# First weight block loaded in two transfers, and one zero multiplication fewer ahead of it, in a two-layer LoRA residual kernel

## The chip, the cores and the metric

The kernel runs on one core of one Trainium2 chip. The metric is device time in microseconds (us) of one execution; lower is better. A core has TensorE (matrix multiplications; weight loads are listed apart, as PEld), VectorE (DVE), ScalarE (ACT), GpSimd (POOL) and SyncE (SP), whose queue issues most of the transfers here.

## What is computed

Two linear layers follow each other, each with a residual and a low-rank correction that is chosen per batch entry by an index (8 batch entries, 256 tokens, width 1024, float32):

```python
base = einsum('bti,oi->bto', x, W0) + b0
x    = x + base + 2 * einsum('btr,bro->bto', einsum('bti,bir->btr', x, A0[idx0]), B0[idx0])
base = einsum('bsd,od->bso', x, W1) + b1
x    = x + base + einsum('bsr,bor->bso', einsum('bsd,brd->bsr', x, A1[idx1]), B1[idx1])
```

## The kernel before, in words

The kernel first multiplies the two weights with each other, (1 + W0) times (1 + W1) in effect, and then applies the product to the tokens of each of the 8 batch entries. Both large products are cut into quadrants of 512 x 512 and combined by sums and differences of quadrants, so that seven quadrant products do instead of eight. The quadrants of the first weight are called u11, u12, u21, u22, those of the second v11 to v22; us3, vt3 and the like are their sums and differences. Every operand is held as a high part (rounded to the format that TensorE multiplies, written by ScalarE as a CAST, "hi") and a low part (the remainder, written by VectorE as a subtraction, "lo"), and a product takes three passes: high x high (line 1127), high x low (line 1131) and low x high (line 1132).

Quadrants u11 and v11 come first, in four blocks k = 0 to 3 of 128 rows x 512 columns (256 KB). The SP queue issues, one after the other, v11 block 0 (line 327), u11 block 0 (line 328), blocks 1 to 3 of both (line 331), then u12, v21 in two halves, u21, v22, v12, u22 (lines 336 and 339). In each block of u11 and v11 the unit matrix has to be added to the 128 x 128 piece on the diagonal. For block 0 this is spread out by hand:

- VectorE (lines 701 to 713) adds the unit matrix to the first 128 columns of v11 and then of u11, once into the high operand (line 707) and once into the raw block (line 708). Then it makes the low parts of v11 and u11, one instruction of 512 columns each (line 712).
- ScalarE (lines 463 to 467) rounds the other 384 columns of v11, then those of u11, into the high operands.
- TensorE (lines 1165 to 1170) fills the time until the data are there with multiplications of zeros: 4 of 128 columns (line 1167), then WARM = 6 of 512 columns (line 1170). Its first real multiplication (row group m = 0, line 1127) waits for the third of the four diagonal additions, m = 1 to 3 wait for ScalarE's part of u11, and the eight low passes of block 0 (lines 1131, 1132) wait for both low parts.

Blocks 1 to 3 go through lines 699 (diagonal), 472 (high) and 718 (low). VectorE's program is one strict list. After the low parts of u12 and of half of v21 it waits for the transfer of u21 (line 941) and makes us3 = u21 - u11 (line 731, combine). Then follow, among others, the low part of the rest of v21, the diagonal of v22, the low part of an adapter factor (line 736, which waits for ScalarE's line 484), vt3, and all low parts up to that of v22 (line 728). TensorE waits for the low part of v22 after it has turned a block by four transposes (line 1153), at the third quadrant product (line 1229). Semaphore counts are kept in `hi` and `lo`, per place; `filled(q, n)` gives the count at which n parts of q are there, from the table PARTS.

Of the kernel before, what the change touches and what calls it, by code (L numbers as in the profile page):

```python
# [8 lines left out]
ALU = mybir.AluOpType  # L9

P = 128
HALF = 512
WARM = 6
WARM_SHORT = 4
DMA = 16

KH = 4
# [10 lines left out]
SLOT = {"u11": 0, "v11": 1, "u12": 2, "v21": 3, "us3": 4, "vt3": 5, "us4": 0, "v22": 2, "us2": 4, "vt2": 0,  # L28
        "us1": 1, "u22": 3, "vt1": 5, "vt4": 2, "d11": 0, "t3": 4, "t2": 5, "d21": 1, "t1": 3, "t4": 2, "d22": 6}


REST = ("12", "21", "22")
PARTS = {"u11": KH, "v11": KH, "u12": 2, "v21": 2, "d21": KH, "d22": KH}


A11, A21, A12, A22, S1, S2, S3, S4 = range(8)
# [3 lines left out]

def lora_pair(nc, xT, U11, V11, W0, W1T, A0, B0T, A1T, B1, b0, b1, idx0, idx1, out):
    B, _, _, QW = xT.shape

    TILES = 4
# [19 lines left out]
    with ExitStack() as ctx:  # L64
# [3 lines left out]
        def sem(name):  # L68
            return ctx.enter_context(nc.semaphore(name))
# [66 lines left out]
        def raw(name):  # L136
            at = UNIT[name]
            return raw_a[:, at, :] if at < 4 else raw_b[:, at - 4, :]

        def raw_k(name, k, n=1):  # L140
            return raw(name)[:, k * HALF:(k + n) * HALF]

        def op(name, part):
            return ops[:, SLOT[name], part, :]

        def op_k(name, part, k, n=1):
            return op(name, part)[:, k * HALF:(k + n) * HALF]
# [48 lines left out]

        warm_set = sem("warm_set")
        landed = {q: sem(f"landed_{q}") for q in ("u12", "u21", "u22", "v12", "v22")}
        v21_landed = [sem(f"landed_v21_{n}") for n in range(KH // GROUP)]
        first_landed = {q: [sem(f"landed_{q}_{g}") for g in range(KH)] for q in ("u11", "v11")}  # L200
        lora_landed = sem("lora_landed")
# [18 lines left out]
        diag_added = sem("diag_added")  # L220
# [4 lines left out]
        hi = [sem(f"hi_of_place{s}") for s in range(7)]  # L225
        lo = [sem(f"lo_of_place{s}") for s in range(7)]
# [57 lines left out]
        def filled(q, n):  # L284

            ahead = list(SLOT)[:list(SLOT).index(q)]
            return n + sum(PARTS.get(p, 1) for p in ahead if SLOT[p] == SLOT[q])

# [4 lines left out]
        def _(sp):  # L293
# [30 lines left out]
                             ).then_inc(stored[name], DMA)  # L324


            sp.dma_start(raw_k("v11", 0), V11[0, :, :]).then_inc(first_landed["v11"][0], DMA)
            sp.dma_start(raw_k("u11", 0), U11[0, :, :]).then_inc(first_landed["u11"][0], DMA)
            for k in range(1, KH):
                for q, src in (("u11", U11), ("v11", V11)):  # L330
                    sp.dma_start(raw_k(q, k), src[k, :, :]).then_inc(first_landed[q][k], DMA)
# [130 lines left out]
        def _(act):  # L462
            def first_block():

                for q in ("v11", "u11"):
                    act.wait_ge(first_landed[q][0], DMA)
                    nc.scalar.copy(op_k(q, 0, 0)[:, P:HALF], raw_k(q, 0)[:, P:HALF]).then_inc(hi[SLOT[q]], 1)

            def high_first(k):
                for n, q in enumerate(("u11", "v11")):  # L470
# [78 lines left out]
            act.dma_start(idx[0:1, B:2 * B], idx1).then_inc(idx_landed, DMA)  # L549
            act.dma_start(idx[0:1, 0:B], idx0).then_inc(idx_landed, DMA)  # L550
            first_block()
            for k in range(1, KH):
                high_first(k)
# [132 lines left out]
        def _(dve):  # L686
# [14 lines left out]
            def first_block():  # L701

                dve.wait_ge(ident_made, 2)
                for q in ("v11", "u11"):
                    dve.wait_ge(first_landed[q][0], DMA)
                    block = raw_k(q, 0)[:, 0:P]
                    nc.vector.tensor_tensor(op_k(q, 0, 0)[:, 0:P], block, ident[:, :], ALU.add).then_inc(diag_added, 1)  # L707
                    nc.vector.tensor_tensor(block, block, ident[:, :], ALU.add).then_inc(diag_added, 1)
                for n, q in enumerate(("v11", "u11")):
                    dve.wait_ge(diag_added, 2 * n + 2)  # L710
                    dve.wait_ge(hi[SLOT[q]], 1)
                    nc.vector.tensor_tensor(op_k(q, 1, 0), raw_k(q, 0), op_k(q, 0, 0), ALU.subtract
                                            ).then_inc(lo[SLOT[q]], 1)

            def low_first(k):
                for q in ("u11", "v11"):
                    dve.wait_ge(hi[SLOT[q]], filled(q, k + 1))
                    nc.vector.tensor_tensor(op_k(q, 1, k), raw_k(q, k), op_k(q, 0, k), ALU.subtract
                                            ).then_inc(lo[SLOT[q]], 1)

# [9 lines left out]
            def combine(q, left, right, how):  # L730
                nc.vector.tensor_tensor(raw(q), raw(left), raw(right), how).then_inc(summed[q], 1)  # L731
# [200 lines left out]
            nc.vector.memset(bias_sum, 0.0).then_inc(zeroed, 1)  # L932
            nc.vector.memset(t_cols[:, :], 0.0).then_inc(zeroed, 1)
            first_block()
            for k in range(1, KH):
                diagonal(k)
                low_first(k)
# [1 line left out]
            low_half("u12", 2)  # L939
            low_half("v21", 0)  # L940
            dve.wait_ge(landed["u21"], DMA)
            dve.wait_ge(lo[SLOT["u11"]], filled("u11", KH))
            combine("us3", "u21", "u11", ALU.subtract)
            low_half("v21", 2)
            add_diagonal("v22", diag_v22)
# [173 lines left out]
        def _(pe):  # L1119
# [6 lines left out]
            def high_pass(u, v, bank, m, k, on_top=False):  # L1126
                return mm(bank[:, :], left(u, 0, k, m), op_k(v, 0, k), start=(k == 0 and not on_top), stop=False,  # L1127
                          skip_group_check=on_top)

            def low_passes(u, v, bank, m, k, on_top=False):  # L1130
                mm(bank[:, :], left(u, 0, k, m), op_k(v, 1, k), start=False, stop=False, skip_group_check=on_top)  # L1131
                return mm(bank[:, :], left(u, 1, k, m), op_k(v, 0, k), start=False, stop=(k == KH - 1),  # L1132
                          skip_group_check=on_top)
# [34 lines left out]
            pe.wait_ge(warm_set, 2)  # L1168
            for _ in range(WARM):
                mm(banks[7][:, :], c_rows[:, 0:P], c_rows[:, 0:HALF], start=True, stop=True)  # L1170


            for k in range(KH):
                if k == 0:

                    pe.wait_ge(diag_added, 3)
                else:
                    pe.wait_ge(hi[SLOT["u11"]], filled("u11", k + 1))
                pe.wait_ge(hi[SLOT["v11"]], filled("v11", k + 1))
                if k < KH - 1:  # L1180
                    for m in range(KH):
                        if k == 0 and m == 1:
                            pe.wait_ge(hi[SLOT["u11"]], filled("u11", 1))
                        high_pass("u11", "v11", a_banks[m], m, k)
                pe.wait_ge(lo[SLOT["u11"]], filled("u11", k + 1))
                pe.wait_ge(lo[SLOT["v11"]], filled("v11", k + 1))
                for m in range(KH):
                    if k == KH - 1:

                        high_pass("u11", "v11", a_banks[m], m, k)  # L1190
                    last = low_passes("u11", "v11", a_banks[m], m, k)
                    if k == KH - 1:
                        last.then_inc(m_done[1], 1)
# [58 lines left out]
            for h in range(NH):  # L1252
                cols = slice(h * HALF, (h + 1) * HALF)
# [235 lines left out]
```

## Time and profile before

| | |
|---|---|
| median of 3 runs | 282.63 us (282.19 to 282.70) |
| the profiled execution, its own time | 281.97 us |
| its span, first to last instruction | 280.4 us |
| TensorE busy | 276.3 us, 99% of the span |
| VectorE busy | 214.5 us, 77% |
| ScalarE busy | 102.0 us, 36% |
| mean granted TensorE clock | 0.999 |

The page sums up one execution. The busy time of TensorE contains the zero multiplications. Of the 281.97 us, 1.57 lie outside the span. The timeline lists instructions by start and duration; a bracket at the end of a line gives the idle time of that engine just before, and what ended it.

### The profile page before, as it was taken

The numbers are of one execution on the slowest core, as the hardware profiler recorded it, in microseconds if no ns is written. First come the engines' busy times: TensorE is split into PE (matmuls) and PEld (weight loads), VectorE is DVE, ScalarE is ACT, GpSimd is POOL, SyncE is SP. The second block draws the span as 40 slices with busy tenths as digits, with TensorE's granted clock in tenths as the row PEclk, the third lists the DMA queues.
The fourth block names the chain that finished last, engine by engine and source line by source line (L and its number), as shares of the span: only waits on it lengthen the run. The fifth ranks groups of instructions, "written<-read, shape, count | busy, mean of one in ns | idle before, by whom it ended". The sixth has DMA issues, their size and how long they took to land.

```text
span 280.4 us, 3861 instructions
## 1 busy us (share of the span) xinstructions
PE 276.3 (99%) x1321; PEld 225.4 (80%) x1321; DVE 214.5 (77%) x321; ACT 102.0 (36%) x141; POOL 19.2 (7%) x45
## 2 busy tenths in 40 slices
PE   8999999999999999999999999999999999999995
PEld 6888888888888886888877888888877888888885
DVE  5779999999899799798972875875772865875413
ACT  4665465352964665404131223132311223132000
POOL 3333200400000001001000000000000000000000
PEclk9999999999999999999999999999999999999999
DMA  7997100200476200383702703703802302203003
GB/s 245 388 411 287 37 1 2 57 19 0 150 269 247 86 2 19 109 314 126 248 15 84 247 29 121 240 6 124 236 1 86 125 0 112 95 2 132 19 0 150
DMA packets 13112, 33.93 MB, mean 121 GB/s; under 512 B 2165, under 2 KB 2421, under 8 KB 13094
## 3 DMA queue, kind: packets, MB, share of 16 engines
q1 hardware_dynamic: 12066, 31.60, 31.8%
q0 software_dynamic: 1024, 2.10, 2.3%
q8 instruction: 10, 0.16, 0.2%
q14 instruction: 8, 0.07, 0.1%
q10 hardware_dynamic: 4, 0.00, 0.0%
HBM read 22.09 MB, written 11.60 MB: 120 GB/s over the span
## 4 chain that ended last, share of the span: by engine, by line
PE 99%; DVE 0%; issue 0%
PE bank L1291 18%; PE bank L1292 18%; PE bank L1293 18%; PE bank L1127 9%; PE bank L1131 9%; PE bank L1132 9%; PE bank L1323 3%; PE bank L1298 3%; PE bank L1159 1%; PE bank L1161 1%; PE bank L1160 1%; PE bank L1147 1%; PE bank L1146 1%; PE bank L1145 1%; PE bank L1170 1%; PE bank L1238 1%
## 5 line engine op out<-in xcount | busy, mean ns | idle before, releaser
L1291 PE MATMUL bank<-ops,late 128*128 128x512 f32 x192 | 75.1, 391 | 0.0
L1292 PE MATMUL bank<-ops,late 128*128 128x512 f32 x192 | 74.8, 390 | 0.0
L1293 PE MATMUL bank<-ops,late 128*128 128x512 f32 x192 | 74.7, 389 | 0.0
L1131 PE MATMUL bank<-ops 128*128 128x512 f32 x112 | 43.8, 391 | 0.0
L1132 PE MATMUL bank<-ops 128*128 128x512 f32 x112 | 43.6, 390 | 0.0
L1291 PEld LDWEIGHTS bank<-ops,late 128*128 128x128 f32 x192 | 36.1, 188 | 8.7 <-issue 1.2
L1293 PEld LDWEIGHTS bank<-ops,late 128*128 128x128 f32 x192 | 36.0, 188 | 7.6
L1292 PEld LDWEIGHTS bank<-ops,late 128*128 128x128 f32 x192 | 36.1, 188 | 7.4
L1127 PE MATMUL bank<-ops 128*128 128x512 f32 x112 | 40.9, 400 | 0.0
L525 ACT CAST late<-rows 128x512 fp32r<-128x512 f32 x24 | 14.7, 620 | 54.7 <-DVE rows L823 29.5
L1127 PEld LDWEIGHTS bank<-ops 128*128 128x128 f32 x112 | 21.5, 192 | 4.7 <-DVE ops L707 0.3
L1132 PEld LDWEIGHTS bank<-ops 128*128 128x128 f32 x112 | 21.2, 189 | 4.5
L1131 PEld LDWEIGHTS bank<-ops 128*128 128x128 f32 x112 | 21.2, 189 | 4.5
L728 DVE TENSOR_TENSOR ops<-raw_a,ops 128x2048 fp32r<-128x2048 f32 x9 | 20.6, 2284 | 0.0
L802 DVE TENSOR_TENSOR late<-rows,late 128x512 fp32r<-128x512 f32 x24 | 16.5, 690 | 4.9 <-ACT late L525 4.8
L479 ACT CAST ops<-raw_a 128x2048 fp32r<-128x2048 f32 x9 | 17.1, 1911 | 7.4 <-DVE raw_a L731 4.6
L909 DVE TENSOR_TENSOR raw_a<-bank,raw_a 128x512 f32<-128x512 f32 x8 | 5.5, 692 | 17.7 <-PE bank L1298 17.6
L479 ACT CAST ops<-raw_b 128x2048 fp32r<-128x2048 f32 x6 | 11.4, 1915 | 6.3 <-DVE raw_b L731 3.7
L728 DVE TENSOR_TENSOR ops<-raw_b,ops 128x2048 fp32r<-128x2048 f32 x6 | 13.6, 2286 | 0.0
L897 DVE TENSOR_TENSOR raw_a<-bank,raw_a 128x512 f32<-128x512 f32 x8 | 5.5, 690 | 8.4 <-PE bank L1293 8.4
L802 DVE TENSOR_TENSOR late<-raw_a,late 128x512 fp32r<-128x512 f32 x15 | 10.1, 687 | 2.0 <-ACT late L525 1.9
L547 ACT COPY raw_a<-bank 128x512 f32<-128x512 f32 x4 | 2.3, 587 | 24.0 <-PE bank L1298 24.0
(175 smaller groups left out, 397.4 us busy)
## 6 DMA issues: line engine op xcount, KB each, us to landing
out<-raw_a SPq DMA_DIRECT2D x27, 256.0 KB, 2.3
raw_a<-xT SPq DMA_DIRECT2D x10, 512.0 KB, 6.8
a<-rb_rows SPq DMA_DIRECT2D x8, 392.0 KB
x_mid<-xT SPq DMA_DIRECT2D x6, 512.0 KB, 6.3
raw_b<-W SPq DMA_DIRECT2D x2, 1024.0 KB, 16.2
rb_rows<-b_hl SPq DMA_DIRECT2D x3, 512.0 KB
rb_rows<-late SPq DMA_DIRECT2D x3, 512.0 KB
raw_b<-V SPq DMA_DIRECT2D x4, 256.0 KB, 3.7
```

The lines of the kernel that those rows point to most:

```text
L479: nc.scalar.copy(op(q, 0), raw(q)).then_inc(hi[SLOT[q]], 1)
L525: nc.scalar.copy(x_op(j, 0), x_raw(j, b)).then_inc(op_hi[j], 1)
L728: nc.vector.tensor_tensor(op(q, 1), raw(q), op(q, 0), ALU.subtract).then_inc(lo[SLOT[q]], 1)
L802: nc.vector.tensor_tensor(x_op(j, 1), x_raw(j, b), x_op(j, 0), ALU.subtract).then_inc(op_lo[j], 1)
L1127: return mm(bank[:, :], left(u, 0, k, m), op_k(v, 0, k), start=(k == 0 and not on_top), stop=False, skip_group_check=on_top)
L1131: mm(bank[:, :], left(u, 0, k, m), op_k(v, 1, k), start=False, stop=False, skip_group_check=on_top)
L1132: return mm(bank[:, :], left(u, 1, k, m), op_k(v, 0, k), start=False, stop=(k == KH - 1), skip_group_check=on_top)
L1291: mm(bank[:, :], hi, t_op(t, 0, k), start=(start and k == 0), stop=False, skip_group_check=not start)
L1292: mm(bank[:, :], hi, t_op(t, 1, k), start=False, stop=False, skip_group_check=not start)
L1293: last = mm(bank[:, :], lo, t_op(t, 0, k), start=False, stop=(k == KH - 1), skip_group_check=not start)
L1298: return mm(bank[:, :], h_stack[b % 2][0:STACK, q * P:(q + 1) * P], rb[b % 2][:, h * HALF:(h + 1) * HALF], start=False, stop=True, skip_gr ...
L1323: last = mm(bank[j * CT:(j + 1) * CT, 0:T], of_b[:, k, :], xr[at][kh][:, :, tok], start=(k < TILES), stop=(k >= KT - TILES))
```

## The change

The transfer of u11 block 0 becomes two: columns 0 to 127 (64 KB, 512 bytes of each row) by itself, and then columns 128 to 511 (192 KB) with a semaphore of their own. WARM goes from 6 to 5. ScalarE's high part of u11 block 0 becomes two instructions (128 and 256 columns), and so does VectorE's low part (256 and 256 columns). TensorE waits for the first piece before m = 1 and for the second before m = 2. u11 now has five parts instead of four, and the counts that others wait for are raised to match.

```diff
-WARM = 6
+WARM = 5
...
-PARTS = {"u11": KH, "v11": KH, "u12": 2, "v21": 2, "d21": KH, "d22": KH}
+PARTS = {"u11": KH + 1, "v11": KH, "u12": 2, "v21": 2, "d21": KH, "d22": KH}
...
+        u11_rest_landed = sem("u11_rest_landed")
...
             sp.dma_start(raw_k("v11", 0), V11[0, :, :]).then_inc(first_landed["v11"][0], DMA)
-            sp.dma_start(raw_k("u11", 0), U11[0, :, :]).then_inc(first_landed["u11"][0], DMA)
+            for cols, done in ((slice(0, P), first_landed["u11"][0]), (slice(P, HALF), u11_rest_landed)):
+                sp.dma_start(raw_k("u11", 0)[:, cols], U11[0, :, cols]).then_inc(done, DMA)
...
-                for q in ("v11", "u11"):
-                    act.wait_ge(first_landed[q][0], DMA)
-                    nc.scalar.copy(op_k(q, 0, 0)[:, P:HALF], raw_k(q, 0)[:, P:HALF]).then_inc(hi[SLOT[q]], 1)
+                for q, done, cols in (("v11", first_landed["v11"][0], slice(P, HALF)),
+                                      ("u11", u11_rest_landed, slice(P, 2 * P)),
+                                      ("u11", u11_rest_landed, slice(2 * P, HALF))):
+                    act.wait_ge(done, DMA)
+                    nc.scalar.copy(op_k(q, 0, 0)[:, cols], raw_k(q, 0)[:, cols]).then_inc(hi[SLOT[q]], 1)
...
-                for n, q in enumerate(("v11", "u11")):
-                    dve.wait_ge(diag_added, 2 * n + 2)
-                    dve.wait_ge(hi[SLOT[q]], 1)
-                    nc.vector.tensor_tensor(op_k(q, 1, 0), raw_k(q, 0), op_k(q, 0, 0), ALU.subtract
-                                            ).then_inc(lo[SLOT[q]], 1)
+                for q, parts, cols in (("v11", 1, slice(0, HALF)), ("u11", 1, slice(0, 2 * P)),
+                                       ("u11", 2, slice(2 * P, HALF))):
+                    dve.wait_ge(diag_added, 2 if q == "v11" else 4)
+                    dve.wait_ge(hi[SLOT[q]], parts)
+                    nc.vector.tensor_tensor(op_k(q, 1, 0)[:, cols], raw_k(q, 0)[:, cols], op_k(q, 0, 0)[:, cols],
+                                            ALU.subtract).then_inc(lo[SLOT[q]], 1)
...
-                    dve.wait_ge(hi[SLOT[q]], filled(q, k + 1))
+                    dve.wait_ge(hi[SLOT[q]], filled(q, k + 1 + PARTS[q] - KH))
...
-            dve.wait_ge(lo[SLOT["u11"]], filled("u11", KH))
+            dve.wait_ge(lo[SLOT["u11"]], filled("u11", PARTS["u11"]))
...
-                    pe.wait_ge(hi[SLOT["u11"]], filled("u11", k + 1))
+                    pe.wait_ge(hi[SLOT["u11"]], filled("u11", k + 2))
                 pe.wait_ge(hi[SLOT["v11"]], filled("v11", k + 1))
                 if k < KH - 1:
                     for m in range(KH):
-                        if k == 0 and m == 1:
-                            pe.wait_ge(hi[SLOT["u11"]], filled("u11", 1))
+                        if k == 0 and m in (1, 2):
+                            pe.wait_ge(hi[SLOT["u11"]], filled("u11", m))
                         high_pass("u11", "v11", a_banks[m], m, k)
-                pe.wait_ge(lo[SLOT["u11"]], filled("u11", k + 1))
+                pe.wait_ge(lo[SLOT["u11"]], filled("u11", k + 2))
```

## Rows read from the trace of the kernel before

**Rows 1.** The page, part 4: the chain that ended last, by engine.
```profile
PE 99%; DVE 0%; issue 0%
```

**Rows 2.** The waits of TensorE's weight loads, whole span: us in total, times, longest.
```profile
PEld bank L1167 <- DVE c_rows L931: 1.3, 1, 1.3
PEld bank L1291 <- issue: 1.2, 3, 0.4
...
PEld bank L1127 <- DVE ops L707: 0.3, 1, 0.3
```

**Rows 3.** The timeline, first 9 us, TensorE: start, duration, instruction, idle before.
```profile
2.22 2.87 PE L1170 MATMUL bank<-c_rows 128*128 128x512 f32 x6
4.65 1.42 PEld L1127 LDWEIGHTS bank<-ops 128*128 128x128 f32 x4 [0.29 <-DVE ops L707]
4.88 1.91 PE L1127 MATMUL bank<-ops 128*128 128x512 f32 x4
6.59 0.59 PE L1131 MATMUL bank<-ops 128*128 128x512 f32 x1
7.02 0.39 PE L1132 MATMUL bank<-ops 128*128 128x512 f32 x1
7.25 0.39 PE L1131 MATMUL bank<-ops 128*128 128x512 f32 x1
```

**Rows 4.** The timeline, 1 to 7 us: SP, VectorE and ScalarE around block 0.
```profile
1.43 0.42 SPq L328 DMA_DIRECT2D raw_a<-U  x1
3.66 0.51 ACT L467 CAST ops<-raw_b 128x384 fp32r<-128x384 f32 x1 [0.60 <-DMA raw_b<-V]
3.73 0.29 DVE L707 TENSOR_TENSOR ops<-raw_b,ident 128x128 fp32r<-128x128 f32 x1 [1.00 <-DMA raw_b<-V]
3.94 0.28 DVE L708 TENSOR_TENSOR raw_b<-raw_b,ident 128x128 f32<-128x128 f32 x1
4.31 0.29 DVE L707 TENSOR_TENSOR ops<-raw_a,ident 128x128 fp32r<-128x128 f32 x1
...
5.32 0.68 DVE L712 TENSOR_TENSOR ops<-raw_a,ops 128x512 fp32r<-128x512 f32 x1
6.24 0.62 ACT L472 CAST ops<-raw_a 128x512 fp32r<-128x512 f32 x1 [1.42 <-DVE raw_a L699]
```

**Rows 5.** Issue to landing: block 0 of v11 (line 327) and of u11 (line 328).
```profile
DMA to landing us min/median/max: 2.6/2.6/2.6
DMA to landing us min/median/max: 2.9/2.9/2.9
```

**Rows 6.** The page, part 6: a transfer of 64 KB: count, size, us to landing.
```profile
a_raw<-A POOLq DMA_DIRECT2D x8, 64.0 KB, 2.0
```

**Rows 7.** Windows: stretch, length, busy per engine, clock, transfer engines' share, GB/s.
```profile
3.00:4.00 1.00, 1.00 (x3) 0.74 (x3) 0.27 (x2) 0.40 (x2) 0.00 (x0) 1.00 1.03 383
12.00:14.00 2.00, 2.00 (x10) 1.65 (x10) 1.46 (x2) 1.99 (x3) 0.77 (x2) 1.00 1.04 422
```

**Rows 8.** The waits of VectorE, 0 to 60 us: total, times, longest.
```profile
DVE raw_a L731 <- DMA raw_b<-W: 1.5, 1, 1.5
DVE ops L718 <- ACT ops L472: 1.5, 3, 0.5
...
DVE ops L723 <- ACT ops L476: 0.5, 1, 0.5
DVE a L736 <- ACT a L484: 0.3, 1, 0.3
```

**Rows 9.** The timeline: u21's transfer, and VectorE's work from its landing to v22.
```profile
6.20 0.46 SPq L339 DMA_DIRECT2D raw_b<-W  x1
18.09 2.29 DVE L731 TENSOR_TENSOR raw_a<-raw_b,raw_a 128x2048 f32<-128x2048 f32 x1 [1.50 <-DMA raw_b<-W]
42.05 2.28 DVE L728 TENSOR_TENSOR ops<-raw_a,ops 128x2048 fp32r<-128x2048 f32 x1
```

**Rows 10.** The timeline, weight loads: the four transposes and the load behind them, twice.
```profile
43.78 0.58 PEld L1153 LDWEIGHTS bank<-ident,g_all 128*128 128x128 f32 x4
44.40 0.19 PEld L1127 LDWEIGHTS bank<-ops 128*128 128x128 f32 x1
102.26 0.58 PEld L1153 LDWEIGHTS bank<-ident,g_all 128*128 128x128 f32 x4
102.81 0.19 PEld L1127 LDWEIGHTS bank<-ops 128*128 128x128 f32 x1
```

## The prediction

> **What bounds the kernel now.** I read the page's chain first: it is TensorE for 99% of the span [rows 1]. So a change is worth what it does to the moment at which TensorE finishes its list. The waits of the weight loads say where that list is held up: 1.3 us at the very start for the first zeros, 0.3 us ahead of the first real multiplication, and a few pauses with no releaser [rows 2]. Seen this way nothing else holds TensorE, and a zero multiplication taken out in front should come off the end. Two closer looks reduce that.
>
> The first is the speed. The first four real multiplications start at 4.88 and the next follows at 6.59, so one of 512 columns takes 1.71/4 = 0.43 us: 1.2 GHz. From 7.02 to 7.25 one takes 0.23: the 2.4 GHz level [rows 3]. The granted clock reads 1.00 in every window, this early one too [rows 7], so the level is read off the spacing. The engine had been at work without a gap since 1.30 [rows 2], and the fast level came between 6.59 and 7.02. The zeros run in the slow stretch. If the moment of the rise stays, what is gained in front of it is slow time, worth 0.23/0.43, about half, at the end.
>
> The second is VectorE. It waits 1.5 us for u21's transfer (issued at 6.20, its consumer starts at 18.09) and then, up to 60 us, only 0.3 us once, for ScalarE's line 484, which itself follows from us3 [rows 8, 9]. So from 18.09 to 44.33 VectorE works through its list, and its last piece there is the low part of v22, 42.05 + 2.28 = 44.33 [rows 9]. TensorE's next weight load starts at 44.40. Behind the four transposes at 102.26 the load follows after 0.55 us; here, behind those at 43.78, after 0.62 [rows 10]. I read the difference, 0.07 us, as a wait for VectorE that the list of waits doesn't show. TensorE is pinned there to the landing of u21, and whatever it gains earlier than that turns into waiting.
>
> **The change part by part.** *One zero multiplication less.* The real work could start 0.43 earlier, at 4.45 instead of 4.88.
>
> *The diagonal piece by itself.* v11 landed at 0.99 + 2.6 = 3.6, u11 at 1.43 + 2.9 = 4.3 [rows 4, 5], and VectorE's addition for u11 starts at 4.31 [rows 4]. The piece of 64 KB is issued at the same 1.43. Bounds: not before v11's 3.6, and at the latest with the whole block, 4.3; its bytes at 383 GB/s [rows 7] are 0.17 us, so I take 3.8. A lone 64 KB takes 2.0 from issue to landing [rows 6], which gives 3.4 and doesn't bind. But VectorE isn't free then: it starts v11's two additions at 3.73 and 3.94, 0.21 apart [rows 4], so u11's comes at 4.15 at the earliest. That is 0.16 before 4.31. The first weight load then starts at 4.65 - 0.16 = 4.49 and the multiplication, 0.23 behind it as now [rows 3], at 4.72. Of the 0.43 taken out, 0.16 is real and 0.27 becomes a pause that wasn't there.
>
> The Trainium skill speaks against such a piece ("DMA: Bandwidth & Descriptors", Rules for kernel authors): many small transfers should be joined, and below 64 KB one pays mostly overhead; its table of measured bandwidth has 0.95 us of transfer time for 64 KB. By that figure the piece would land at about 4.5, later than the whole block does now, which is the third rival below with a larger size.
>
> *The rest of the block.* It is issued one SP instruction later, at 1.86 (0.42 per issue [rows 4]), and lands between 4.31 (bytes in the same order) and 1.86 + 2.9 = 4.76; I take 4.45. ScalarE's 384 columns take 0.51 and 512 take 0.62 [rows 4], 0.11 per 128, so the 128 columns for m = 1 take 0.29, ready at 4.74. The load for m = 1 can start up to about 4.92 without delay. At the late bound it is ready at 5.05, and the gain for the later row groups is gone. The 256 columns take 0.40, ready at about 5.15, before m = 2 needs them at about 5.35.
>
> *The low parts.* An instruction of 128 columns takes 0.29 and one of 512 takes 0.68 [rows 4], so 256 take 0.42 and two of them 0.16 more than one whole. VectorE starts them earlier by as much as its diagonal work moved (0.15), so they end at about 5.95, against 6.00 now. The low passes can start 0.16 earlier than at present, so this just holds. Costed at nothing; without that cover it is 0.1 us. The extra 0.16 on VectorE goes into its waits for ScalarE behind it, 1.5 us in three [rows 8].
>
> *The front in sum.* Up to 7.02 TensorE starts (7.02 - 4.72)/0.43 = 5.4 real multiplications instead of 5, and 0.38 of one at the fast level is 0.09 us.
>
> *The SP queue.* Every transfer behind block 0, the rest of both quadrants and the six that follow, is issued about 0.43 later. u21 goes from 6.20 to 6.65 and lands near 18 because the transfer engines are full until then: share 1.03 and 1.04 [rows 7]. So the later issue costs nothing; its cover is some 11 us of queued bytes. If the queue ran empty it would cost the whole 0.43. What does count is the number of packets. The same bytes now come in 256 row pieces instead of 128, eight more for each of the 16 transfer engines. The blocks with rows of 2 KB run at 383 GB/s, which is 16 x 2048/383 = 86 ns per piece, and those with 4 KB pieces at 422, 155 ns [rows 7]. A straight line through both is 16 ns per piece plus 34 per KB. Eight times 16 is 0.13 us, which I take; the bounds are 0 and eight whole 2 KB pieces, 0.69. Less than nothing is excluded: no byte is saved.
>
> By the Trainium skill (same page, Why small descriptors are slow) a packet costs about 3 cycles extra, which at the page's 850 MHz is an estimate of 0.03 us for eight. No row prices a single small packet; the sum by it would be +0.03 instead of +0.13.
>
> *The sum.* u21 lands 0.13 later, VectorE's whole run up to 44.33 moves with it, and TensorE's load at 44.40 goes to 44.53. The 0.09 from the front only lengthens the wait there. Net +0.13 us. This is against the profiled execution, 281.97 (span 280.4 and 1.57 around it). The median is 0.66 longer; nothing shows where those runs spend it. I put the difference on the median: 282.76, rounded to **282.8**. A measurement of this kernel can tell about 0.2%, 0.57 us, from no change.
>
> **The rivals.** *The pin doesn't hold* (the 0.07 is an accident of the transposes, or in most runs TensorE reaches 44 us later than VectorE anyway, as the 0.66 may mean). Then the front's gain arrives: 0.09, or with data in time for all of the 0.43, one fast multiplication, 0.23. Time 282.4 to 282.55. For it: no listed wait at 44.40. Against it: 44.33 and 44.40 lie as close together as a releaser and its waiter do.
>
> *The pause delays the fast level.* This is the case on the slow side. Until now TensorE worked without a gap from 1.30 to the rise at 7.0, 5.7 us. Now there is a pause at 4.45 to 4.72. If it makes the engine begin anew, the rise comes 5.7 after 4.72, at 10.4, so 3.4 us later, and half of that is lost: +1.7, less 0.07 of waiting and the 0.09: +1.55. Time 284.2. It decides from any pause that the clock's monitor counts as idleness; against it is that 0.27 is 5% of 5.7 us, and no row shows a pause ahead of the rise.
>
> *The split brings nothing earlier*: both pieces land with or behind the old block (at 4.3 to 4.5). The pause grows to 0.43 to 0.6, real work starts up to 0.2 later than now, TensorE is 0.1 late after the rise and 0.03 later than the pin allows. Time 282.7 to 282.9, no change that can be told.
>
> *Packets at the dear bound.* Eight whole pieces, or a queue that runs short with the later issues: u21 0.6 to 0.7 later. Time 283.3.
>
> Faster by over 0.57 has no mechanism in these rows: the front can give 0.23, and only if the pin gives way.
>
> **How the numbers follow.** Forecast 0.50; no pin 0.20; split brings nothing 0.11; late fast level 0.12; dear packets 0.05; 0.02 for a faster case that I don't see. The late level and most of the dear packets are slower; scatter adds a little on each side (the three runs lie 0.5 apart): faster 0.06, same 0.78, slower 0.16. The range goes from 282.2 (no pin, the most it gives, and 0.2 of scatter) to 283.4 (dear packets); it leaves out the late level and the unseen case, 0.14, and some scatter.
>
> **What would show it.** Right: the first real weight load near 4.49, waiting for VectorE's line 707, the first multiplication near 4.72 with some 0.27 of idle TensorE before it; spacing of 0.43 up to about 7.0; the u21 wait of VectorE ending near 18.2; the low part of v22 ending near 44.46 and the load behind the transposes near 44.5, more than 0.62 after them. Wrong: spacing of 0.43 lasting beyond 7.5 (late level); the load 0.55 behind the transposes and the end 0.1 or more earlier (no pin); u11's first piece landing after 4.2; or u21 landing before 18.0 or after 18.5.

## The result, and the profile of the changed kernel

| | before | changed |
|---|---|---|
| median | 282.25 us (281.68 to 283.65, 16 runs) | 282.95 us (282.39 to 283.91, 16 runs) |
| ratio | | 1.0023, 95% interval 1.0013 to 1.0033 |
| profiled execution, its own time | 281.97 us | 282.81 us |
| its span | 280.4 us | 281.2 us |

The changed kernel is 0.23% slower by the ratio, 0.65 us, with an interval of 0.37 to 0.93 us (the medians lie 0.70 apart). The forecast was +0.13 us and a time of 282.8: the sign and the place were right, the size was five times too small. That the time of 282.8 is only 0.15 off is partly luck. It was built on 282.63, the median of three runs of the kernel before; with more runs that median is 282.25, and this error of 0.38 covers most of the missing 0.5 us.

The front first. These are rows of the timeline of the changed kernel, 1 to 8 us, all engines (start, duration, instruction; line 712 is 707 of before, 472 is 467, 1133 is 1127, 1137 and 1138 are 1131 and 1132, 718 is 712):

```profile
1.44 0.89 SPq L331 DMA_DIRECT2D raw_a<-U  x2
3.80 0.29 DVE L712 TENSOR_TENSOR ops<-raw_b,ident 128x128 fp32r<-128x128 f32 x1 [1.07 <-DMA raw_b<-V]
4.21 0.28 DVE L712 TENSOR_TENSOR ops<-raw_a,ident 128x128 fp32r<-128x128 f32 x1
4.55 0.29 PEld L1133 LDWEIGHTS bank<-ops 128*128 128x128 f32 x1 [0.61 <-DVE ops L712]
4.55 2.53 PE L1133 MATMUL bank<-ops 128*128 128x512 f32 x4
5.08 0.60 ACT L472 CAST ops<-raw_a 128x128 fp32r<-128x128 f32 x2 [0.85 <-DMA raw_a<-U]
5.43 0.93 PEld L1133 LDWEIGHTS bank<-ops 128*128 128x128 f32 x3 [0.59 <-ACT ops L472]
5.49 0.76 DVE L718 TENSOR_TENSOR ops<-raw_a,ops 128x256 fp32r<-128x256 f32 x2 [0.18 <-ACT ops L472]
6.88 0.63 PE L1137 MATMUL bank<-ops 128*128 128x512 f32 x1
7.31 0.52 PE L1138 MATMUL bank<-ops 128*128 128x512 f32 x1
7.67 0.40 PE L1137 MATMUL bank<-ops 128*128 128x512 f32 x1
```

The diagonal piece does what it should: VectorE adds its unit matrix at 4.21, directly behind v11's two additions and not behind a transfer, and the first weight load starts at 4.55, 0.10 earlier than before [rows 3]. Then the rest of the block is late. ScalarE can start on it at 5.08, where it used to have the whole block at 4.31, and the weight load for m = 1 waits 0.59 us for it. So TensorE is 0.29 behind at its first low pass (6.88 against 6.59 [rows 3]). The spacing falls from 0.43 to 0.23 near 7.6 here, not at 7.0. (The row of the first four multiplications starts at 4.55, together with the load. Up to 6.88 they take 2.33 us, where four at 0.43 take 1.71, so about 0.6 us is lost inside that row.)

The transfer engines lose much more. The window of 3 to 4 us of the changed kernel, to be held against the first of [rows 7]:

```profile
3.00:4.00 1.00, 1.00 (x3) 0.75 (x3) 0.20 (x1) 0.33 (x2) 0.00 (x0) 1.00 0.88 211
```

The rate is 211 GB/s where it was 383, and the busy share of the transfer engines is 0.88 where it was 1.03, so they were not full all the time, as the prediction had them. The SP queue is late, too. It issues u21 here:

```profile
5.70 1.65 SPq L339 DMA_DIRECT2D raw_a<-W1T  x2
7.39 0.67 SPq L342 DMA_DIRECT2D raw_b<-W  x1
```

That is 1.19 later than the 6.20 of before [rows 9] and 0.74 later than the 6.65 of the prediction: the two issues for v21 in front of it take 1.65 us. Around 44 us, the timeline of the changed kernel shows u21's consumer, VectorE's low part of v22, the four transposes and the load behind them:

```profile
18.91 2.29 DVE L737 TENSOR_TENSOR raw_a<-raw_b,raw_a 128x2048 f32<-128x2048 f32 x1 [0.80 <-DMA raw_b<-W]
...
42.88 2.28 DVE L734 TENSOR_TENSOR ops<-raw_a,ops 128x2048 fp32r<-128x2048 f32 x1
...
44.23 0.58 PEld L1159 LDWEIGHTS bank<-ident,g_all 128*128 128x128 f32 x4
...
45.23 0.19 PEld L1133 LDWEIGHTS bank<-ops 128*128 128x128 f32 x1 [0.42 <-issue]
```

Against [rows 9, 10]: u21 is consumed at 18.91 instead of 18.09, 0.82 later; VectorE's last piece ends at 42.88 + 2.28 = 45.16 instead of 44.33; the load starts 0.07 behind it, as before, at 45.23 instead of 44.40; and the span is 0.8 longer. TensorE's own lateness at the transposes is 0.45 (44.23 against 43.78) and hides in the wait. The list of waits names the releaser wrongly: "issue" stands where VectorE is meant.

### The profile page after: what moved, and what is told of

Its sections match the earlier page's. It is cut to its first block, busy times and chain, and to the rows that moved or that the text cites. A ratio compares the mean times of both kernels' runs of the same rounds, so it can differ in the third digit from the quotient of the medians.

```text
span 281.2 us, 3863 instructions
## 1 busy us (share of the span) xinstructions
PE 276.8 (98%) x1320; PEld 224.9 (80%) x1320; DVE 214.7 (76%) x322; ACT 101.8 (36%) x142; POOL 19.3 (7%) x45
## 4 chain that ended last, share of the span: by engine, by line
PE 97%; DMA 1%; SPq 0%; issue 0%; DVE 0%; ACT 0%
PE bank L1297 18%; PE bank L1298 18%; PE bank L1299 18%; PE bank L1133 9%; PE bank L1137 9%; PE bank L1138 9%; PE bank L1329 3%; PE bank L1304 3%; PE bank L1165 1%; PE bank L1167 1%; PE bank L1166 1%; PE bank L1152 1%; PE bank L1151 1%; PE bank L1153 1%; DMA raw_a<-U 1%; PE bank L1244 1%
```

## The experiments

All twelve, in three sets; each set has its own runs of the kernel before. They are called e1 to e12 in the order in which they stand here. Each has one profile, of one execution; the ratios come from all its runs. The theory going in: the loss is u21's later landing, passed on by VectorE's list and the wait near 44 us, and what makes u21 late is the number of pieces.

**The split alone.** Six zeros, no split of the high and low instructions; everything waits for both pieces.

```diff
-            sp.dma_start(raw_k("u11", 0), U11[0, :, :]).then_inc(first_landed["u11"][0], DMA)
+            for cols in (slice(0, P), slice(P, HALF)):
+                sp.dma_start(raw_k("u11", 0)[:, cols], U11[0, :, cols]).then_inc(first_landed["u11"][0], DMA)
...
-                    act.wait_ge(first_landed[q][0], DMA)
+                    act.wait_ge(first_landed[q][0], 2 * DMA if q == "u11" else DMA)
...
-                    dve.wait_ge(first_landed[q][0], DMA)
+                    dve.wait_ge(first_landed[q][0], 2 * DMA if q == "u11" else DMA)
```

> The kernel before with u11 block 0 in two transfers (128 and 384 columns) and nothing else: six zero multiplications, one high and one low instruction per block, everything waits for both pieces. Theory (pieces shorter than 2 KB cost the transfer engines nearly as much time as whole ones, u21 lands later, and TensorE is pinned to it near 44 us): both pieces landed near 5.0 instead of 4.3, VectorE's wait for u21 ends near 18.8 instead of 18.09, TensorE's load behind the first four transposes starts near 45.1 instead of 44.40, time 0.5 to 0.8 us over the kernel before (ratio 1.002 to 1.003). Rival (the loss is made at the front, by the pause and the late row groups, or by the split high and low instructions, not by u21): u21 at most 0.2 later, time within 0.3 us of the kernel before.

Measured: 283.69 against 282.55 us, ratio 1.0035 (1.0017 to 1.0052). The split of the transfer is enough for the loss. The profiled run, 284.20 us, shows more than was expected, though. Its timeline, ScalarE's and TensorE's rows at the front, u21's consumer, and the two loads near 46 us:

```profile
3.64 0.52 ACT L468 CAST ops<-raw_b 128x384 fp32r<-128x384 f32 x1 [0.58 <-DMA raw_b<-V]
5.28 0.51 ACT L468 CAST ops<-raw_a 128x384 fp32r<-128x384 f32 x1 [1.12 <-DMA raw_a<-U]
5.63 2.08 PE L1128 MATMUL bank<-ops 128*128 128x512 f32 x4 [0.54 <-DVE ops L708]
...
10.49 0.60 PE L1133 MATMUL bank<-ops 128*128 128x512 f32 x1
10.91 1.09 PE L1128 MATMUL bank<-ops 128*128 128x512 f32 x4
...
19.45 2.29 DVE L732 TENSOR_TENSOR raw_a<-raw_b,raw_a 128x2048 f32<-128x2048 f32 x1 [1.39 <-DMA raw_b<-W]
...
46.07 0.58 PEld L1154 LDWEIGHTS bank<-ident,g_all 128*128 128x128 f32 x4
46.63 0.19 PEld L1128 LDWEIGHTS bank<-ops 128*128 128x128 f32 x1
```

The block lands 1.64 after v11's, TensorE pauses 0.54, and the spacing stays at 0.43 until about 10.9. In this run u21 isn't what holds TensorE: VectorE's low part of v22 ends at 43.40 + 2.28 = 45.68, but the transposes start only at 46.07 and the load follows after the natural 0.56. This is the rival of the late fast level in one execution: the load starts at 46.63, 0.9 us later than VectorE alone would have it, and the span of 282.6 is 2.2 over the first of before.

**One zero less alone** (`WARM = 5`, nothing else).

> The kernel before with WARM = 5 instead of 6 and nothing else. Theory (pin): the first real multiplication stays near 4.88 behind a pause of about 0.43, u21 still lands near 18, time within 0.2 us of the kernel before. Rival (a pause ahead of the rise of the clock delays the fast level): spacing of 0.43 lasts beyond 7.5, up to 10 us, and the time is 0.3 to 1.6 us longer.

Measured: 282.69 against 282.55, ratio 1.0002 (0.9988 to 1.0015): no difference. The first real weight load waits 0.7 us for the same addition of VectorE, so the removed zero becomes waiting. The spacing falls at about 7.6, so the late level doesn't show here. Two rows of the profile mattered for the theory. First, u21's consumer in the timeline of this kernel, which has no split:

```profile
18.88 2.29 DVE L731 TENSOR_TENSOR raw_a<-raw_b,raw_a 128x2048 f32<-128x2048 f32 x1 [0.97 <-DMA raw_b<-W]
```

It comes as late as in the changed kernel, and the time is unchanged, so u21's landing scatters by some 0.8 us from one execution to the next, and one profile of each kernel can't measure its shift. Second, the waits of TensorE's weight loads show another place, near 110 us, where TensorE waits for VectorE (copies of adapter factors, line 851) and which neither profile compared at first shows; this run, 283.52 us by its own time, pays 0.7 us for it:

```profile
PEld bank L1323 <- DVE aa L851: 1.5, 1, 1.5
```

**u21 ahead of v21's second half**, in the changed kernel and in the kernel before. It takes one wait away at its source: u21 then has 512 KB less in front of it.

```diff
-            for q in ("u12", "v21", "u21", "v22", "v12", "u22"):
+            for q in ("u12", "v21 0", "u21", "v21 1", "v22", "v12", "u22"):
                 src = W0 if q[0] == "u" else W1T
-                if q == "v21":
-                    for n, done in enumerate(v21_landed):
-                        sp.dma_start(raw_k(q, n * GROUP, GROUP), src[REST.index(q[1:]), n, :, :, :].rearrange(
-                            "p k n -> p (k n)")).then_inc(done, DMA)
+                if q[:3] == "v21":
+                    n = int(q[4])
+                    sp.dma_start(raw_k("v21", n * GROUP, GROUP), src[REST.index("21"), n, :, :, :].rearrange(
+                        "p k n -> p (k n)")).then_inc(v21_landed[n], DMA)
                     continue
```

> The changed kernel with u21's transfer issued ahead of the second half of v21's (512 KB, about 1.25 us at 410 GB/s). Theory (pin): VectorE's wait for u21 ends near 17.7 instead of 18.91 and its list runs that much earlier, the load behind the first transposes follows after 0.55 instead of 1.00 us, and what stays is the later front of TensorE alone (its transposes came at 44.23 against 43.78): time 0.3 to 0.4 us shorter than the changed kernel, still 0.2 to 0.4 over the kernel before. Rival (the pin is not what holds it): no change against the changed kernel, within 0.15 us.

Measured: 282.88 against 282.55, ratio 1.0012 (0.9994 to 1.0031). The middle is half of the changed kernel's loss, as expected; the interval holds both that and the rival. The profile misses the expected values: u21 is consumed at 18.40 and not at 17.7, without a wait, but VectorE then waits 0.47 us for v22's transfer, its last piece ends at 45.28, and the load starts at 45.35, 0.65 behind the transposes and not 0.55. VectorE's list still holds TensorE there.

> The kernel before with u21's transfer issued ahead of the second half of v21's. Theory (pin): the load behind the first transposes follows after 0.55 instead of 0.62 us and the profiled run is 0.07 us shorter; over many runs, whose spread comes in part from when u21 lands, 0.1 to 0.4 us shorter than the kernel before. Rival (the runs' spread comes from the front or the clock): within 0.1 us.

Measured: 281.95 against 282.55, **ratio 0.9973 (0.9959 to 0.9988)**, 0.6 us under the kernel before. That is more than the 0.1 to 0.4 expected. Nothing but the order of two transfers changed, no byte and no instruction elsewhere, so the time does hang on when these transfers land, as the pin requires. The timeline of this kernel shows u21's consumer with no wait for its transfer, a new wait for v22's, VectorE's last piece, and the load following the transposes after 0.55:

```profile
17.89 2.28 DVE L731 TENSOR_TENSOR raw_a<-raw_b,raw_a 128x2048 f32<-128x2048 f32 x1
...
21.83 0.90 DVE L691 TENSOR_TENSOR raw_a<-raw_a,ident 128x128 f32<-128x128 f32 x4 [0.53 <-DMA raw_a<-W1T]
...
42.33 2.28 DVE L728 TENSOR_TENSOR ops<-raw_a,ops 128x2048 fp32r<-128x2048 f32 x1
...
44.30 0.58 PEld L1153 LDWEIGHTS bank<-ident,g_all 128*128 128x128 f32 x4
44.85 0.19 PEld L1127 LDWEIGHTS bank<-ops 128*128 128x128 f32 x1
```

VectorE is done at 44.61, TensorE starts its load 0.24 later, by its own pace. This single profile ran 282.91 us and is no picture of the gain, since u21 was consumed early in the first profile of before, too; and TensorE waits 1.2 us for line 851 near 110 in it. The median over the runs is what shows the gain. No profile shows how it comes about: in the three kernels with this order (this one, e3 and e8) VectorE's last piece ends at 44.61, 45.28 and 45.25, none before the 44.33 of the first profile of before. What the three do share is that u21 no longer makes VectorE wait and that v22's transfer does, for 0.5 to 0.7 us. So the new order puts v22's transfer in u21's place on VectorE's list, and in e3 and e8 that list still decides when the load starts.

**What makes the transfers slow?** Three variants of the split, each with everything else as before (the waits as in the first experiment), and one more test of the front. By rows, `U11[0, part, :]` for `part in (slice(0, P // 2), slice(P // 2, P))`:

> The kernel before with u11 block 0 in two transfers of 64 rows of the full 2 KB each, so one issue more but the same 128 pieces. Theory (what costs is the number of pieces, each some 70 to 100 ns of an engine whether 512 B or 2 KB long): the block has landed 0.6 to 0.8 us after v11's, as unsplit (0.62 to 0.80 so far), 3 to 5 us runs at 264 GB/s or more, time within 0.1% of the kernel before. Rival (the additional transfer itself, its issue and its completion, costs it): landed 1.3 or more after v11's, time 0.2% to 0.4% longer, as with the split by columns.

Measured: 283.15 against 282.59, ratio 1.0026 (1.0010 to 1.0042). The block landed 0.96 after v11's (ScalarE's casts at 3.86 and 4.82), later than the unsplit 0.62 to 0.80 known by then and far from 1.3, and yet the time is as long as with the split by columns. This fits neither expectation as a whole: the number of pieces can't be all.

By even columns, `(slice(0, 2 * P), slice(2 * P, HALF))`:

> The kernel before with u11 block 0 in two transfers of 256 columns (pieces of 1 KB, 256 of them). Theory (number of pieces): as with 128 and 384, landed 1.3 to 1.7 after v11's, time 0.2% to 0.4% over the kernel before. Rival (the odd piece of 1536 B, or the short one of 512 B, is what is slow): landed under 1.1 after v11's, time within 0.1%.

Measured: 283.28 against 282.59, ratio 1.0027 (1.0012 to 1.0042), landed 1.81 after v11's. The odd length of 1536 bytes isn't the cause.

By 128 and 384 columns, both pieces contiguous in memory:

```diff
+            for cols, at in ((slice(0, P), 0), (slice(P, HALF), P * P)):
+                n = cols.stop - cols.start
+                sp.dma_start(raw_k("u11", 0)[:, cols], U0[at:at + P * n].rearrange("(p n) -> p n", n=n)
+                             ).then_inc(first_landed["u11"][0], DMA)
...
+        "U0": np.concatenate([u_first[0, :, :P].ravel(), u_first[0, :, P:].ravel()]),
```

> The 128/384 split alone (as in e1), but both pieces of the block laid out contiguously in memory by the host, so that no transfer skips over bytes: the same 256 pieces. Theory (number of pieces): no change against e1, landed 1.3 to 1.7 after v11's, time 0.2% to 0.4% over the kernel before. Rival (reading with a stride in memory is what is slow): landed under 1.0 after v11's, time within 0.1% of the kernel before.

Measured: 283.85 against 282.59, ratio 1.0048 (1.0031 to 1.0064), landed 1.93 after v11's. The stride isn't the cause either.

The order of e4 together with `WARM = 5`:

> The kernel before with u21's transfer ahead of v21's second half (as e4) and WARM = 5, without any split: with the pin near 44 us gone, does the front count? Theory: the real work can't start earlier than VectorE's addition for u11 (about 4.65 for its weight load), so it is the same as e4, 0.2% to 0.3% under the kernel before. Rival: the missing zero lets real work start up to 0.2 us earlier: 0.1 us under e4 at most. Third: the pause makes the fast level late in some runs: over e4 by 0.1% or more.

Measured: 282.10 against 282.59, ratio 0.9984 (0.9975 to 0.9994). The interval overlaps e4's, which was taken beside other runs. A gain from the missing zero doesn't show here either; whether it costs something can't be told from these two. The expectation took the pin as gone, which it isn't in this profile: VectorE waits 0.68 us for v22's transfer, ends at 45.25, and the load follows at 45.32.

**One more issue, or more pieces?** First, one more transfer of 64 bytes, needed by nobody, behind u11 block 0:

```diff
+            sp.dma_start(tiny[0:1, :], b1[0:1, 0:16]).then_inc(tiny_landed, DMA)
...
+            sp.wait_ge(tiny_landed, DMA)
             sp.wait_ge(zeroed, 1)
```

> The kernel before with one more transfer of 64 bytes (one piece, needed by nobody) issued behind u11 block 0, so every later issue comes about 0.45 us later and nothing else changes. Theory A (the later issue itself costs, as the split by rows suggests, which has no piece more and was 0.26% longer): time 0.15% to 0.35% over the kernel before, u21 consumed at 18.7 or later. Theory B (only pieces cost; queued bytes cover the later issue): within 0.1% of the kernel before.

Measured: 282.88 against 282.28, ratio 1.0014 (1.0000 to 1.0029). u21's consumer starts at 19.21 in the profile. The block itself landed 0.55 after v11's, as early as ever, while the rate of 2 to 5 us is 219 GB/s. Theory A got its later u21, but e2 had it nearly as late (18.88) with no transfer more, so this one profile proves little; for the time the interval reaches down to nothing.

Second, the changed kernel with the second piece issued by ScalarE's queue:

```diff
-            for cols, done in ((slice(0, P), first_landed["u11"][0]), (slice(P, HALF), u11_rest_landed)):
-                sp.dma_start(raw_k("u11", 0)[:, cols], U11[0, :, cols]).then_inc(done, DMA)
+            sp.dma_start(raw_k("u11", 0)[:, 0:P], U11[0, :, 0:P]).then_inc(first_landed["u11"][0], DMA)
...
+            act.dma_start(raw_k("u11", 0)[:, P:HALF], U11[0, :, P:HALF]).then_inc(u11_rest_landed, DMA)
```

> The changed kernel with the second piece of u11 block 0 (columns 128 to 511) issued from ScalarE's queue, near 1.75 us, so the SP queue has no issue more than in the kernel before. Theory A (the later issue costs): the loss goes, within 0.1% of the kernel before. Theory B (the pieces cost): as the changed kernel, 0.15% to 0.35% over the kernel before.

Measured: 283.08 against 282.28, ratio 1.0022 (0.9998 to 1.0047), u21 consumed at 18.93. The SP queue has no issue more than in the kernel before, and in the profile u21 is no earlier than in the changed kernel. That speaks against one more issue on SP as the whole cause. It doesn't rule it out: the interval of the time just reaches theory A's 1.000, and the profile is one execution. In it SP comes to u21 at 7.01 instead of 6.20, although it has no issue more, so its issues can be held up in another way.

**Both kernels again**, to see how far a single profile can be trusted.

> The kernel before once more, under its own name: how wide is the scatter of a ratio, and of one profile? Both theories: ratio 1.000, within 0.1%. In the profile, u21's consumer at 18.1 if that place in the first profile is typical, at 18.5 or later if the first profile was an early one; the moment at which the spacing falls from 0.43 to 0.23 anywhere between 5 and 9 us.

Measured: 282.33 against 282.28, ratio 1.0005 (0.9991 to 1.0019). u21 consumed at 18.15, so the first profile was no exception. Here the fast level was there by 5 us, and TensorE only waited longer, as the timeline's loads show:

```profile
43.33 0.58 PEld L1153 LDWEIGHTS bank<-ident,g_all 128*128 128x128 f32 x4
44.46 0.19 PEld L1127 LDWEIGHTS bank<-ops 128*128 128x128 f32 x1 [0.55 <-issue]
```

TensorE reached the transposes 0.45 earlier than in the first profile [rows 10], the load started 0.06 later than there, with VectorE's list (42.11 + 2.28 = 44.39), and the span is 280.7 against 280.4. A head start of TensorE is worth nothing here.

> The changed kernel once more: ratio 1.0013 to 1.0033 as at first; both pieces of u11 block 0 landed 1.3 to 1.9 us after v11's, and the rate of 2 to 5 us at 200 to 240 GB/s. If its second landing comes within 1.0 of v11's, the cost of the pieces was an accident of single profiles.

Measured: 283.17 against 282.28, ratio 1.0029 (1.0012 to 1.0047), the loss again; 2 to 5 us ran at 214 GB/s, and the second piece landed 2.05 after v11's block. The profiled run, 284.37 us, is of the same kind as e1's. Its waits of TensorE's matrix side and the timeline rows at the change of level:

```profile
PE bank L1133 <- ACT ops L472: 0.8, 1, 0.8
```
```profile
10.60 0.62 PE L1138 MATMUL bank<-ops 128*128 128x512 f32 x1
11.03 1.12 PE L1133 MATMUL bank<-ops 128*128 128x512 f32 x4
```

The pause of 0.78 us, for the second piece, and the spacing of 0.43 until 11.0 put the transposes at 46.24 and the load at its natural 0.55 behind, 46.79.

### What the profiles say together

| kernel | u11 block 0 whole, us after v11's | u21 consumed | load near 45 us | span minus that load |
|---|---|---|---|---|
| before, first | 0.65 | 18.09 | 44.40 | 236.0 |
| before, again | 0.74 | 18.15 | 44.46 | 236.2 |
| one zero less | 0.62 | 18.88 | 45.18 | 236.7 |
| tiny transfer | 0.55 | 19.21 | 45.51 | 236.0 |
| split by rows | 0.96 | 18.71 | 45.02 | 236.0 |
| split 128/384 | 1.64 | 19.45 | 46.63 | 236.0 |
| split 256/256 | 1.81 | 18.86 | 45.18 | 236.0 |
| split, contiguous | 1.93 | 18.86 | 45.17 | 236.0 |
| changed, first | 1.36 | 18.91 | 45.23 | 236.0 |
| changed, again | 2.05 | 19.81 | 46.79 | 236.0 |
| changed, by ScalarE | 1.82 | 18.93 | 45.24 | 236.0 |

The first column is the distance of ScalarE's casts for v11 and u11. The three kernels with u21 moved forward are left out; their differences are 236.1 to 236.4. Two things can be read. The end follows the load near 45 us at a distance of 236.0, so what is decided by then is decided. It is more only where TensorE waits 0.8 us or longer for VectorE's line 851 near 110: 1.5 us in "one zero less" (236.7), 1.2 in e4 (236.4), 1.0 in the second profile of before (236.2) and in e3 (236.2), 0.8 in e8 (236.1). VectorE's list holds TensorE there a second time. At the load near 45 us itself, VectorE decides in all of these but two, the split 128/384 and the second profile of the changed kernel, where TensorE itself is late; of the three left out it decides in e3 and e8. And in every profile with one transfer more, by rows, by columns or just 64 bytes, u21 is consumed at 18.7 or later (eight of eight), while without it two of three are near 18.1.

The rate of the transfers from 2 to 12 us goes along with it: 359 and 352 GB/s where u21 is consumed near 18.1, 314 to 338 where it is at 18.7 to 19.5, and 298 at 19.81. But a low rate isn't special to the kernels with one transfer more. From 2 to 8 us they moved 245 to 300 GB/s, and the five without it 349, 322, 304, 286 and 282. So the profiles tie u21's landing to the early rate; that one transfer more makes a low rate more frequent is read from the medians, not shown by the profiles.

## Why the prediction was right or wrong, point by point

**The pin: right.** TensorE is held near 44 us by VectorE's list, and that list by u21's landing, or by v22's once u21 is moved forward. The changed kernel's load stands 0.07 behind VectorE as predicted, the spans moved by the same 0.8 as u21's consumer, the second profile of the kernel before turned a 0.45 us head start of TensorE into waiting, and the 0.27% that e4 gains from the order of two transfers agrees with it. The first rival (no pin) falls. What the prediction didn't see is the second such place near 110 us.

**One zero less: right.** Worth nothing, by e2, within 0.15%.

**The diagonal piece: right.** Predicted, VectorE's addition at 4.15 and the load at 4.49; measured 4.21 and 4.55, both 0.06 late because v11's own start was 0.07 later. The piece itself landed at 1.44 + 2.5 = 3.9, against the 3.8 taken and the 4.5 of the prediction's other estimate. The multiplication was put 0.23 behind the load, at 4.72; the rows have both at 4.55, so the predicted pause of 0.27 shows only as the load's wait of 0.61.

**The rest of the block: wrong.** Bounded at 4.31 to 4.76, taken as 4.45; ScalarE got it at 5.08, and in other kernels with the column split (e3, e10, e12) at 5.20, 5.55 and 5.82. The bound "1.86 + 2.9" assumed that the piece travels no longer than the whole block did; it took 3.2. So m = 1 lost 0.59 at the very place where 0.09 was to be gained, and the low parts ended at 6.25 instead of 5.95. Behind the pin all this costs nothing, unless the fast level comes late.

**The packets: the term that was mis-sized.** I took "16 ns per piece", 0.13 us, from a line through two rates. The u21 of the first two profiles came 0.82 later, past even the dear bound of 0.69, and the time 0.65. The forecast's number came from here, and so did its error. The line wasn't sound: its early rate, 383 GB/s, is 322 in the same window of the kernel before again, and with that rate the same line gives 48 ns per piece and 0.39 us. Nor can the count of pieces be the whole term, since e5, with no piece more, cost 0.26%. The Trainium skill's figure ("DMA: Bandwidth & Descriptors", Why small descriptors are slow), an estimate of 0.03 us from its three cycles, is further off still; the measurement decides. The Trainium skill's rule against small transfers (same page, Rules for kernel authors) agrees in its direction with the measured loss.

**"So the later issue costs nothing": not sustained.** Eleven microseconds of queued bytes should have covered it, but the split by rows, which adds no piece, cost 0.26%, and one idle transfer of 64 bytes 0.14% (0 to 0.29%). The sum also had the lateness wrong: u21 was to be issued at 6.65 and was at 7.39, and the engines that were to be full had a share of 0.88. In e10, with no issue more on SP, u21 was still at 18.93. What the slow kernels have in common is one more transfer in the first 3 us. By which mechanism it slows the engines between 2 and 8 us, whether the late issues are a cause or a result of it, and how the cost divides between pieces and transfer, stays open.

**The pause and the fast level: wrong to give it 0.12 as an all-or-nothing case.** It is a matter of the single execution. In five profiles TensorE stopped for 0.5 to 0.9 us after the zeros or after its first real multiplication; in three of them (e6, e7, e10) the short spacing was there directly after the pause, in two (e1, e12) it came only at 10.9 and 11.0, later than in any of the others (8.8 at most), and these two have the longest spans, 282.6 and 282.8. That fits a level put off by a pause that falls ahead of it. Against it stand the changed kernel's first profile and e3: both lose about 0.6 us inside their first four multiplications, waiting for the second piece, and have the short spacing from 7.6 and 7.8. No run held everything else fixed, so the cause is argued, not shown. It may be a reason why kernels with the split reach 284 to 285 us in the later sets, where the kernel before stays under 283.9; how much of the 0.65 us comes from such executions, and not from u21, isn't known.

**The signs and the chances.** One of the signs named for being wrong came, u21 at 18.91 where 18.5 was the limit, and the rise near 7.6 just passed another, 7.5. 0.16 for slower was too little, since the measured +0.23% is at the line drawn at 0.2%. The dear-packet rival, given 0.05, has about the shift of u21 and the size that were measured, though not its reason, the pieces alone.

## What to carry to other kernels

Before trimming the front of a kernel, look for the first place further on where the bottleneck engine waits for another one, by comparing one sequence of instructions with its repetition elsewhere (0.62 against 0.55 us here): up to that place, only what releases the other engine counts. A transfer that is cut in two for an earlier start of its first part can delay its second part and what is queued behind, as it did here. If one of those feeds the pin, the order of the transfers is the better lever: moving u21 ahead of half of v21 gave 0.27%, and the split took 0.23%. After such a move look which transfer holds the list next; here it was v22's. And with early transfer rates that scatter, repeat both profiles before putting a number on a shift of some tenths.

## What was not expected of the hardware

- The moment at which the spacing of 512 columns falls from 0.43 (1.2 GHz) to 0.23 (the 2.4 GHz level) lay anywhere between 5 and 11 us in profiles whose first multiplication always started at 1.30. For the kernel before it was 7.0 in one execution and under 5 in the next.
- The transfer rate of 2 to 5 us was 326 and 289 GB/s in two executions of the kernel before, and 289, 251 and 261 in the three other kernels without a further transfer (e2, e4, e8). With one transfer of 64 bytes more it was 219, with the split by rows 262, and with the column splits 201 to 240, 287 once. From 12 to 18 us it is 412 to 417 in all fourteen profiles.
- Two halves of 64 rows landed together 0.96 us after v11's block, an unsplit block 0.55 to 0.96 (six profiles, the 0.96 in e8); two column pieces of the same bytes took 1.34 to 2.05, contiguous in memory (1.93) or not.
